# Row sums of the second query half: added up on GpSimd, then one ones-product instead of eight

## The reference

```python
q = (x @ w_q.T).reshape(Bc, Tc, H, D).transpose(0, 2, 1, 3)   # the same for k and v
scores = jnp.einsum('bhqd,bhkd->bhqk', _rope(q), _rope(k)) * SCALE
scores = jnp.where(tok_mask[None, None], scores, -jnp.inf)    # causal by blocks of 64
attn = jax.nn.softmax(scores, axis=-1)
ctx = jnp.einsum('bhqk,bhkd->bhqd', attn, v)
```

## Time and profile before

| what | us |
|---|---|
| median of three runs | 710.92 |
| the profiled execution | 710.02 |
| its span in the trace | 708.2 |
| the four groups' B stages, first sequence | 144.4 to 321.3 |
| PE busy, share of the span | 84% |
| POOL busy, share of the span | 22% |

### The profile page before, as it was taken

One profiled execution on the slowest core, in us unless ns is written; L12 is line 12 of the kernel. 1 busy time (PEld: TensorE's weight loads), 2 busy tenths in 40 slices (PEclk: granted clock), 3 DMA queues, 4 the chain that ended last, 5 costly groups with the idle time before them and its releaser, 6 DMA issues.

```text
span 708.2 us, 9858 instructions
## 1 busy us (share of the span) xinstructions
PE 592.3 (84%) x3554; PEld 219.0 (31%) x3554; DVE 443.2 (63%) x878; ACT 294.4 (42%) x597; POOL 157.2 (22%) x131
## 2 busy tenths in 40 slices
PE   0384878799999999998656687888999999999895
PEld 0232433333323222233324343333323323222252
DVE  5998459777677772014868854987776768400464
ACT  1711211146456666743306121113555557685232
POOL 1800422213123010104316124222222210000232
PEclk9987999899999999999967899998999999999899
DMA  8420332221221100000410023222212210000003
GB/s 311 184 26 0 111 112 68 82 76 46 68 69 55 37 2 1 2 1 1 178 59 1 0 66 114 89 91 67 68 46 71 66 46 2 1 1 1 1 1 118
DMA packets 35033, 41.41 MB, mean 58 GB/s; under 512 B 3026, under 2 KB 27730, under 8 KB 34986
## 3 DMA queue, kind: packets, MB, share of 16 engines
q1 hardware_dynamic: 31962, 36.23, 16.1%
q10 hardware_dynamic: 3024, 4.56, 1.8%
HBM read 23.88 MB, written 16.78 MB: 57 GB/s over the span
## 4 chain that ended last, share of the span: by engine, by line
PE 60%; DVE 28%; DMA 4%; issue 3%; ACT 2%; POOL 2%; SPq 0%; DVEq 0%; ACTq 0%
PE bank L701 11%; PE bank L673 10%; PE bank L761 9%; PE bank L752 9%; PE bank L685 7%; PE bank L644 6%; DVE rot L573 5%; DVE rmax L556 4%; PE bank L636 4%; DVE xl L500 3%; DVE stats L475 3%; DVE big L491 3%; PE bank L729 3%; DVE t L566 2%; DVE xs L510 2%
## 5 line engine op out<-in xcount | busy, mean ns | idle before, releaser
L556 DVE TENSOR_REDUCE rmax<-bank 128x1 f32<-128x512 f32 (+3 forms) x384 | 200.2, 554 | 95.9 <-PE bank L685 91.8
L403 ACT ACTIVATE big<-bank 128x512 f32<-128x512 f32 (+3 forms) x384 | 175.9, 488 | 148.9 <-PE bank L673 146.1
L685 PE MATMUL bank<-kst,qst 104*128 104x512 f16 (+3 forms) x384 | 126.0, 337 | 24.8 <-DVE rmax L556 19.4
L673 PE MATMUL bank<-qst,kst 106*128 106x512 f16 (+3 forms) x384 | 120.9, 332 | 2.3 <-ACT big L403 1.2
L333 POOL TENSOR_TENSOR t<-t,rot 128x512 f32<-128x512 f32 x32 | 40.5, 1266 | 200.3 <-DVE rot L573 200.3
L752 PE MATMUL bank<-big,ones 128*32 128x512 f32 (+3 forms) x768 | 81.8, 498 | 0.9 <-ACT cf L423 0.9
L761 PE MATMUL bank<-big,vs 128*32 128x512 f32 (+3 forms) x768 | 81.8, 498 | 0.0
L673 PEld LDWEIGHTS bank<-qst,kst 106*128 106x128 f16 x384 | 34.6, 96 | 143.0 <-ACT big L403 99.2
L343 POOL TENSOR_TENSOR cl<-cf,ch 128x512 f16<-128x512 f32 x16 | 18.5, 1157 | 203.1 <-ACT ch L429 203.1
L701 PE MATMUL bank<-xh,wh 128*128 128x512 f16 x128 | 42.0, 426 | 18.6 <-DVE xl L519 14.2
L636 PE MATMUL bank<-wt,xh 128*128 128x512 f16 x128 | 37.4, 420 | 23.6 <-DVE xl L500 23.6
(11 more groups left out here) (70 smaller groups left out, 618.8 us busy)
## 6 DMA issues: line engine op xcount, KB each, us to landing
spread<-rhl SPq DMA_DIRECT2D x32, 256.0 KB, 2.2
qst<-spread SPq DMA_DIRECT2D x16, 384.0 KB, 3.8
kst<-spread SPq DMA_DIRECT2D x16, 384.0 KB, 3.8
vs<-in_L_attn_x_dram SPq DMA_DIRECT2D x4, 1024.0 KB, 6.6
spread<-rhl SPq DMA_DIRECT2D x32, 128.0 KB, 2.1
out_dram<-xs ACTq DMA_DIRECT2D x16, 256.0 KB, 2.0
xs<-in_L_ffn_weight_dram SPq DMA_DIRECT2D x1, 1024.0 KB, 8.4
kst<-in_L_attn_w_q_dram SPq DMA_DIRECT2D x1, 1024.0 KB, 14.1
```

The costliest lines, as they stand in the source:

```text
L403: nc.scalar.activation(probs[:, st % P_PLACES, h, 0:n], pb[u % 2][:, 0:n], ACT.Exp, scale=EXP_SCALE).then_inc(s_eb, 1)
L556: nc.vector.tensor_reduce(rmax[:, at:at + 1], pa[u % 3][:, 0:n], AX.X, ALU.max, negate=True).then_inc(s_max, 1)
L673: nc.tensor.matmul(pb[u % 2][:, 0:n], kst[0:ROWS_B, g % SETS, h, j * P:(j + 1) * P], qst[0:ROWS_B, g % SETS, h, q0:q0 + n], start=True, st ...
L685: nc.tensor.matmul(pa[u % 3][:, 0:n], qst[0:ROWS_A, g % SETS, h, i * P:(i + 1) * P], kst[0:ROWS_A, g % SETS, h, half * HALF:half * HALF + ...
```

## The change

For the second query half POOL adds the probabilities of the eight key tiles head by head into a tile `total` (128 x 4 x 512, fp32): the first addition takes j = 0 and j = 1, the next six add one tile each. That is 28 additions a group. The seven later ones-products and the first fall away for this half; one ones-product of four heads on `total` takes their place, 10 steps after the first unit of j = 7. The first half keeps its four ones-products, two steps later than before; all value products come four steps later. ACT also waits for the additions before it reuses a place of `probs`. `total` lies in rows 4 to 7 of `xs`, so these 1 MB go to a DRAM tensor `resid` before the loop and back near its end. The output projection in the loop starts four steps later and the loop is six steps longer.

```diff
-SUM_LAG, PV_LAG = 5, 7
+SUM_LAG, PV_LAG = 7, 11
+ADD_LAG, TOTAL_LAG = 5, 10
+LAST_ADD = 7
+ADDS = GH * LAST_ADD
-LAST_STEP = STEPS * (GROUPS + 2) + B_START + PV_LAG + 2
+LAST_STEP = STEPS * (GROUPS + 2) + B_START + max(PV_LAG + 2, TOTAL_LAG + 4) + 1
-O_START = STEPS * (GROUPS + 1) + B_START + 28
+O_START = STEPS * (GROUPS + 1) + B_START + 32
+BACK_STEP = STEPS * (GROUPS + 1) + B_START + GH * (4 + LAST_ADD) + TOTAL_LAG + 1
...
+        total = xs[:, 4:8, :]
+        resid = nc.dram_tensor("resid", (P, 4, C), F32, kind="Internal").ap()
...
+                sp.wait_ge(s_y, b * 24 + 16)
+                sp.dma_start(resid, xs[:, 4:8, :]).then_inc(s_spill, 16)
                 for k in range(LAST_STEP):
+                    if k == BACK_STEP:
+                        sp.wait_ge(s_spill, 16 * b + 16)
+                        sp.wait_ge(s_total, (b + 1) * GROUPS)
+                        sp.dma_start(xs[:, 4:8, :], resid).then_inc(s_back, 16)
...
+                    if (t := b_unit(k - ADD_LAG)) and t[3] and 1 <= t[4] <= LAST_ADD:
+                        g, st, h, half, j, q0, n = t
+                        done = (b * GROUPS + g) * ADDS + GH * (j - 1) + h
+                        pool.wait_ge(s_eb, b * 192 + STEPS * g + GH * st + h + 1)
+                        if j == 1:
+                            pool.wait_ge(s_spill, 16 * b + 16)
+                            if g:
+                                pool.wait_ge(s_total, b * GROUPS + g)
+                            first = probs[:, (st - 1) % P_PLACES, h, 0:n]
+                        else:
+                            pool.wait_ge(s_add, done - GH + 1)
+                            first = total[:, h, HALF - n:HALF]
+                        pool.tensor_tensor(total[:, h, HALF - n:HALF], first, probs[:, st % P_PLACES, h, 0:n], ALU.add
+                                           ).then_inc(s_add, 1)
...
+                        if st >= 4 + P_PLACES or g and st < 4:
+                            j_old, g_old = (st - 4 - P_PLACES, g) if st >= 4 else (st + 4, g - 1)
+                            if j_old <= LAST_ADD:
+                                act.wait_ge(s_add, (b * GROUPS + g_old) * ADDS + GH * max(j_old, 1))
...
-                        act.wait_ge(s_sum, b * 48 + 12 * c[0] + 4 + 8 * c[1])
+                        act.wait_ge(*((s_total, b * GROUPS + c[0] + 1) if c[1] else (s_sum, b * GROUPS + c[0] + 1)))
...
+                    if r >= 4:
+                        dve.wait_ge(s_back, 16 * b + 16)
...
+                    if (t := pv_step(k, TOTAL_LAG)) and t[2] and t[3] == LAST_ADD:
+                        g, st, half, j, q0, n = t
+                        pe.wait_ge(s_add, (b * GROUPS + g + 1) * ADDS)
+                        pe.wait_ge(s_ln, b * 8 + 2 * g + 1)
+                        for h in range(GH):
+                            last = nc.tensor.matmul(psum[h * D:(h + 1) * D, :], ones[:, 0:D], total[:, h, :], start=True,
+                                                    stop=True, skip_group_check=True)
+                        last.then_inc(s_total, 1)
+                    if (t := pv_step(k, SUM_LAG)) and t[2] == 0:
+                        g, st, half, j, q0, n = t
+                        pe.wait_ge(s_eb, b * 192 + STEPS * g + GH * (st + 1))
+                        if j == 0 and g:
+                            pe.wait_ge(s_ln, b * 8 + 2 * g)
+                        for h in range(GH):
+                            last = nc.tensor.matmul(psum[h * D:(h + 1) * D, q0 - half * HALF:HALF], ones[:, 0:D],
+                                                    probs[:, st % P_PLACES, h, 0:n], start=(j == 0), stop=(j == 3),
+                                                    skip_group_check=True)
```

More of the change, by code:

```diff
@@ L178, in macaron @@
         s_sum = sem("s_sum")
+        s_add = sem("s_add")
+        s_total = sem("s_total")
+        s_spill = sem("s_spill")
+        s_back = sem("s_back")
         s_pv = sem("s_pv")
@@ L743, in _ @@
                         transposed += 1
-                    if t := pv_step(k, SUM_LAG):
+                    if (t := pv_step(k, TOTAL_LAG)) and t[2] and t[3] == LAST_ADD:
[15 more added lines that the diff above has]
+                                                    skip_group_check=True)
+                        if j == 3:
+                            last.then_inc(s_sum, 1)
+                    if t := pv_step(k, PV_LAG):
                         g, st, half, j, q0, n = t
@@ L748, in _ @@
                             pe.wait_ge(s_vs, b * TILES + TILES)
[L749 to L757, removed]
                         if j == 0 and (g or half):
```

## The result

790.13 us against 710.54 for the kernel before, four runs each: the ratio is 1.112, with an interval of 1.110 to 1.114. The profiled execution took 790.2, its span is 788.3 us. I had forecast 760 and a range of 735 to 788. The direction was right, the size was not: about 80 us slower in place of 49.

The account below looks back on a forecast made before the run. PE was taken to set the pace; its 45.3 us saved would become waiting, while longer group periods added 24.8 us a sequence, 49.6 in all, to the profiled 710.0: about 760 us, range 735 to 788.

Parts of the forecast that it names:

- The ring: B step 20, POOL's additions, product at step 54, next group's step 20: longer periods add 24.8 us a sequence, 49.6 in all.
- The additions: POOL's 28 additions a group for the second half: 28.5 us (27.5 to 29.5), wide ones 1.27 us each.
- It always has data: During the additions PE is ahead, so POOL, at 1.27 us a unit slower than PE's step, never lacks input.
- W: POOL's work from step 20 to the last addition, other queue entries included: 36.8, 33.1, 30.0, 29.7 us for the four groups.
- They take turns: DVE's short two-SBUF-input operations alternate with POOL's additions, adding 1.0 us to groups 0 and 1, 0.3 to group 2.
- The clock: PE runs at half clock after waiting for the last additions: 1.7 us lost a stop, lower end none.
- The value products later, at nothing: Value products four steps later still precede the scores whose exponential waits for their place; counted as costing nothing.
- the logarithm's wait: Next first half's j = 0 ones-product waits on PE for the logarithm: 0.8 us with projections, 1.2 without.
- Spill and way back at nothing: 1 MB out before the loop and back near its end: covered, though a longer read could cost 0 to 2 us a sequence.
- Rival 1: POOL keeps up, the last addition is ready at step 54 and PE stays the bound: 672 us, 4 in 100.

Follow-up runs that it names:

- e1_adds_first: Changed kernel with the additions three steps earlier in GpSimd's queue (ADD_LAG 2 instead of 5), ahead of the step 26 rope addition: 776.0 us, ratio 1.095.
- e3_short_adds: Changed kernel with every addition from the third key tile on cut to 128 columns, sums incomplete, all waits kept: 728.4 us, ratio 1.024.
- e11_short_again: Changed kernel with additions cut to 128 columns from the third tile on, ones-products nine steps behind, additions two: 713.8 us, ratio 1.006.

## Why the prediction was half right

The same terms, forecast and measured, in the first sequence (us). "GpSimd" runs from the start of its first addition to the start of the product on `total`, "PE" from there to the next group's first addition:

| term | forecast | measured |
|---|---|---|
| first addition of group 0 | 165.2 | 165.89 |
| GpSimd, group 0 | 36.8 | 42.0 |
| PE, 0 to 1 | 19.2 | 17.9 |
| GpSimd, group 1 | 33.1 | 39.6 |
| PE, 1 to 2 | 15.3 | 16.1 |
| GpSimd, group 2 | 30.0 | 30.8 |
| PE, 2 to 3 | 13.5 | 16.5 |
| group 3 to its last logarithm | 31.8 | 31.4 |
| sum of what was missed | | + 15.3 |

15.3 us a sequence are the 30.6 that lie between 49.6 and the measured 80.2 of the profiled executions.

- **The ring**: right. Sign, mechanism, place and the waits named for it (the product on `total` for the additions, 3.3 and 4.4 us in groups 2 and 3; in groups 0 and 1 PE was later itself and waited 0.57 us and not at all) are in the trace. With the three extra terms edited out the kernel costs 6.7%, 48 us; I had put the ring at 49.6. The terms are not quite the same ones, so I take that as agreement in size and not as proof.
- **The additions**: right. 28.5 us forecast; the rows of groups 2 and 3 give 4.95 + 22.96 = 27.9. The narrow ones took 1.00, 0.73 and 0.455 us, above my 0.98, 0.68, 0.39. The estimate from the Trainium skill, page "GPSIMD Engine Reference", section "Elementwise — side-by-side cycle accounting", 1.00, 0.73 and 0.46, agrees with these to 0.01. The wide ones followed each other at 1.24, which made up for the narrow ones.
- **"It always has data"**: this step failed, and in the rows it is the largest. I checked data against GpSimd's pace, not the order of its queue. The rope addition of step 26, which I did list among W's terms, gets its input only when PE is there. I counted its 1.27 us and not the wait: 5.43 us in groups 0 and 1 and 1.48 before the last rope of group 0, 12.3 us a sequence, beside 15.3 missed in all (other terms came out smaller than forecast). What the runs show of it is less: with the ready additions ahead of the rope, some 12 us of the launch came back, 6 a sequence. The earlier trace rows and the rope's place in the code had it all: eight steps or so of PE behind step 20, while GpSimd had only one addition ahead of the rope.
- **"They take turns"**: failed. The earlier trace rows shows turns, with long operations on both sides. Of the three short operations only two have two SBUF inputs; the middle one (L587) has one. In the loop a short operation of DVE was held 7.81 us (up to 8.03) and the additions were not delayed by it. My 1.0, 1.0 and 0.3 us on GpSimd were not there; PE was 2.85 us late in group 1 in their place.
- **The clock**: right in kind, off in size. 1.7 us a boundary forecast, 1.0, 2.4 and 3.9 read from the stretches. After the stop of 2.9 us in the earlier trace rows PE had dense work; here scattered scores and two fp32 groups in a step followed, and in group 2 the clock, which had fallen at about 307, stood at 0.50 until 323, 11 us from the start of the product on `total`.
- **The value products later, at nothing**: failed. I checked that no wait was violated and not the spacing. Alone the shift costs 4.5%. I had priced the logarithm's wait (0.8 to 1.2 us), but not that lags of 7 and 11 put both fp32 groups in one step. In the change, where only the first half has ones-products, moving them two steps gives 14 us back. In the table that sits in PE's way, mostly in "2 to 3", and there part of it is clock. By the runs this step cost no less than the one on GpSimd's data: undoing each in part gave back 14 us and 12.
- **Spill and way back at nothing**: right. The tail's rows show the way back landed before it was needed, and GpSimd's first additions waited for ACT alone (31.1 us in all), never for the spill.
- **Rival 1's price**: wrong. 672 us took a ones-product's 0.99 us in the chain for its worth. The kernel with short additions and both distances mended stands at 713.8, and against the kernel with the same lags and all ones-products 45 us less of PE's work gave 10. PE was dense, but its products also covered the round trip through ACT and two banks: the waits for exponentials show some 15 of the missing 35 us, those for `cf` some 4. How much of the rest is the clock was not separated.

The range ended 2 us short. Its contributions were all widths of terms that I had; no end of it allowed for a term that was missing.

## What to carry to other kernels

A dense engine is not yet a bound: where its work alternates with another engine through two buffers, taking out an item leaves a hole in its place, so price the round trip that remains and not the item. When work moves to a slack engine, write down its queue in order around the new work and put beside each entry when its input is ready; a short entry whose input is late costs its wait, not its length. And when a distance in steps is changed, look at it modulo the period of the loop.

## What was unexpected in the hardware

A DVE operation on 4 elements, 0.16 us in most instances, took up to 8.03 us beside a run of GpSimd additions, and up to 11.97 us in e1_adds_first. It was a `tensor_tensor` with two SBUF inputs; with that removed, a `tensor_scalar` from SBUF to SBUF took up to 7.01 us, while a `tensor_reduce` from SBUF stayed below 0.17. The additions were not slowed (1.27 us). Where they were cut short (0.45 us each, in shorter runs), the same `tensor_tensor` took at most 0.46 and 0.52 us, in e3_short_adds and e11_short_again. Why some such operations got their turn after one addition (1.2 us) and others only at the end of the run, the runs don't show.
